# A four-layer graph network: A added to the scores on VectorE, row constants dropped, and two small sums moved to GpSimd

## The reference

```
# layer 0, h = relu(layernorm(x)), adj is A (256 x 256)
s1 = h @ (A[:, :128]).T            # by i: "U" in the kernel, bias b_lin is added
s2 = h @ (A[:, 128:]).T            # by j: "W" holds -s2
pre = s1[:, :, None, :] + s2[:, None, :, :] + b_lin
e = einsum('bije,e->bij', where(pre >= 0, pre, 0.2 * pre), a) + A
x = x + sigmoid(softmax(e, axis=2) @ h)
# layer 1
x_h = elu(h @ Wi + bi)
e = sigmoid(a_tgt[:, :, None] + a_src[:, None, :] + be) * mask
agg = e @ x_h ;  self_part = x_h * sum(e, axis=-1)
recv = elu(concat(agg, self_part) @ Wn + bn)
x = x + concat(recv, x_h) @ Wm + bm
```

## Time and profile before

| | us |
|---|---|
| median of 3 runs (5992.98 to 6012.51) | 5996.21 |
| the profiled execution, its own time | 5989.9 |
| its span, first to last instruction | 5988.1 |
| PE busy | 5885.9 (98%) |
| ACT busy | 5269.2 (88%) |
| POOL busy | 4916.4 (82%) |
| DVE busy | 4837.7 (81%) |

### The profile page before, as it was taken

The page is one execution under the profiler, slowest core; times in us unless marked ns, Lnnn a source line. Parts: engine busy times, 40 slices in busy tenths (PEclk is TensorE's granted clock), DMA queues, the critical chain, the costliest instruction groups (busy, mean ns, idle before and its releaser), DMA issues.

```text
span 5988.1 us, 128923 instructions
## 1 busy us (share of the span) xinstructions
PE 5885.9 (98%) x41812; PEld 2318.3 (39%) x41812; DVE 4837.7 (81%) x9171; ACT 5269.2 (88%) x12793; POOL 4916.4 (82%) x10392
## 2 busy tenths in 40 slices
PE   8999999999999999999999999999999999999997
PEld 2333333333334333333333333333433333333334
DVE  8978887888887888878888788888888887888873
ACT  8988898899988899888999889998889988899983
POOL 9988888888888888888888888888888888888880
PEclk9999999999999999999999999999999999999998
DMA  0000000000000000000000000000000000000000
GB/s 13 5 3 7 7 7 6 3 6 7 7 6 3 7 6 7 7 2 7 6 7 7 6 3 6 7 7 6 3 7 6 7 6 3 7 6 7 7 5 6
DMA packets 44353, 36.62 MB, mean 6 GB/s; under 512 B 4721, under 2 KB 39410, under 8 KB 43506
## 3 DMA queue, kind: packets, MB, share of 16 engines
q1 hardware_dynamic: 43506, 26.50, 1.5%
HBM read 9.71 MB, written 8.39 MB: 3 GB/s over the span
## 4 chain that ended last, share of the span: by engine, by line
PE 94%; ACT 2%; DVE 1%; POOL 1%; issue 1%; DMA 0%; SPq 0%; POOLq 0%; ACTq 0%; DVEq 0%
PE S L1015 58%; PE R L957 15%; PE S L957 6%; PE W L957 5%; PE R L1157 3%; PE PA L957 2%; ACT ring L812 2%; PE R L1165 1%; POOL ring L507 1%; PE PB L957 1%; PE S L1006 1%; PE S L1008 1%; DVE ring L613 1%; PE PB L1042 1%; PE PA L1023 0%
## 5 line engine op out<-in xcount | busy, mean ns | idle before, releaser
L507 POOL TENSOR_SCALAR ring<-W,U 128x256 f32<-128x256 f32 x9664 | 4686.4, 503 | 713.8 <-PE S L1015 642.2
L812 ACT ACTIVATE ring<-W,U 128x256 f32<-128x256 f32 x10272 | 4244.1, 503 | 13.3 <-PE S L1015 13.2
L1015 PE MATMUL S<-ring,a_window 128*32 128x512 f32 x32768 | 3750.1, 596 | 12.8 <-POOL ring L507 7.3
L613 DVE TENSOR_TENSOR ring<-U,W 128x512 f32<-128x512 f32 (+1 forms) x3840 | 3209.2, 862 | 155.5 <-PE S L1015 117.4
L1015 PEld LDWEIGHTS S<-ring,a_window 128*32 128x32 f32 x32768 | 952.2, 110 | 2269.6 <-issue 2245.4
L608 DVE TENSOR_TENSOR ring<-U,W 128x256 f32<-128x256 f32 x2464 | 993.6, 408 | 0.0
L957 PE MATMUL R<-mT,W 128*128 128x512 f32 (+1 forms) x640 | 339.1, 611 | 2.7 <-ACT mT L916 2.7
L957 PE MATMUL R<-AT,h 128*128 128x256 f32 x1260 | 316.8, 395 | 2.7 <-ACT h L928 2.1
L748 DVE SCALAR_TENSOR_TENSOR rh<-tr,h3T 128x512 f32<-128x512 f32 (+1 forms) x165 | 114.1, 692 | 240.2 <-ACT tr L919 240.2
L957 PEld LDWEIGHTS R<-AT,h 128*128 128x128 f32 x1260 | 230.4, 193 | 129.7 <-issue 100.6
L478 POOL TENSOR_TENSOR minus_mean<-mv,minus_one 128x4 f32<-128x4 f32 (+1 forms) x160 | 31.6, 197 | 272.3 <-DVE mv L676 216.8
(11 more groups left out here) (186 smaller groups left out, 4238.6 us busy)
## 6 DMA issues: line engine op xcount, KB each, us to landing
X<-in_x SPq DMA_DIRECT2D x64, 128.0 KB, 2.4
X_held<-X SPq DMA_DIRECT2D x32, 256.0 KB, 2.3
out<-OUT SPq DMA_DIRECT2D x64, 128.0 KB, 1.9
raw<-in_L_gnn_w_w SPq DMA_DIRECT2D x3, 128.0 KB
A<-in_adj SPq DMA_DIRECT2D x1, 256.0 KB, 2.7
Wn<-in_L_gnn_Wn SPq DMA_DIRECT2D x1, 128.0 KB
Wm<-in_L_gnn_Wm SPq DMA_DIRECT2D x1, 128.0 KB
rawu<-in_L_gnn_u_w SPq DMA_DIRECT2D x2, 64.0 KB
```

The costliest lines, as they stand in the source:

```text
L507: last = gp.tensor_scalar(ring[:, place, g, half * N:(half + 1) * N], W[:, y, c], LARGEST, U[:, y, c, i:i + 1], ALU.min, ALU.max)
L613: piece = dve.tensor_tensor(ring[:, place, g:g + groups].rearrange("p g (h j) -> p g h j", h=NB), u.unsqueeze(3).to_broadcast([P, groups, ...
L812: last = act.activation(ring[:, place, g, half * N:(half + 1) * N], W[:, y, c], ACT.Relu, bias=U[:, y, c, i:i + 1], scale=-1.0)
L1015: last = pe.matmul(S[y][g * ROWS:(g + 1) * ROWS, :], a_window[:, c, ROWS - 1 - row:2 * ROWS - 1 - row], ring[:, place, g], start=False, st ...
```

## The change

1. The weights `lin_w` are now 128 columns wide, the plain product of A's second half with `a`, the same for every row. One matmul of 512 columns, with H0T read twice, sets up `S`. `by_max`, `w_lin`, `A_bias` and their making are gone, and so are the one-column matmuls for `lin_i`.
2. ScalarE's blocks are relu(W - U[i]) in place of relu(U[i] - W). They differ from max(W, U[i]) by U[i], which is the same for every j of a row and so cancels in the softmax. ScalarE needs -U as its bias: VectorE makes `U_minus` (128x512) at `PRE["evacuate"]`, where it had copied `lin_i`.
3. VectorE's maximum pass becomes two passes of 128x256. Each adds A to the scores, negates, writes the result to SBUF (`neg_score`) and keeps the row's minimum (`neg_max`). The small step that made `exp_bias` is gone. ScalarE's exp reads `neg_score` with scale -1.
4. In layer 1, GpSimd adds the two halves of the edge weights (`edge_sum`), so the row sums take one matmul of 512 columns in place of four of 256. GpSimd adds bm + 0.5 to X1 (`X1_shifted`), so the four matmuls with one row of ones are gone.
5. `stage_costs` has two new costs for GpSimd, so `SHARES` changes: 403 blocks for VectorE, 298 for GpSimd, 323 for ScalarE. 45 of the 128 lots have another split.

```diff
-L1 = dict(project=26, ...
+L1 = dict(shift=22, halves=37, project=26, ...
...
+    put(pool, L1, 0, shift=13, halves=13)
...
-            gp.memset(by_max[:], 1.0).then_inc(mask_ones, 1)
...
+            def layer1(t, turn):                       # GpSimd
+                pair = turn.at(1, 0)
+                if t == L1["shift"]:
...
+                    need(gp, x2_ready, turn.at(1, -1))
+                    gp.wait_ge(x1_ready, turn.at(2, 0))
+                    gp.tensor_tensor(X1_shifted[:], X1[:], bm_half[:].unsqueeze(1).to_broadcast([P, 4, P]), ALU.add).then_inc(x1_shifted, 1)
+                if t == L1["halves"]:
+                    gp.wait_ge(edge_ready, pair)
+                    gp.tensor_tensor(edge_sum[:].rearrange("p (y n) -> p y n", y=2), edge[:, :, 0], edge[:, :, 1], ALU.add).then_inc(edge_halves, 1)
...
                 if p == PRE["evacuate"]:                # VectorE
-                    dve.wait_ge(uw_psum, value)
-                    dve.tensor_copy(lin_i[:, y], PA[:, N:N + NB])
+                    dve.wait_ge(u_ready, value)
+                    dve.tensor_scalar(U_minus[:, y], U[:, y], -1.0, None, ALU.mult).then_inc(u_minus_ready, 1)
...
                     dve.wait_ge(freed[RING - 1], lots_done)
-                    dve.tensor_reduce(neg_max[:], S[y][:].rearrange("p (r j) -> p r j", r=NB), AXIS.X, ALU.max,
-                                      negate=True).then_inc(max_ready, 1)
-                    one_piece()
-                    dve.wait_ge(max_ready, value)
-
+                    need(dve, prob_ready, value - 1)
+                    dve.memset(score_carrier[:], 0.0)
                     for r in range(NB):
-                        last = dve.scalar_tensor_tensor(exp_bias[:, r:r + 1], neg_max[:, r:r + 1], lin_i[:, y, r:r + 1],
-                                                        lin_i[:, y, r:r + 1], ALU.subtract, ALU.add)
-                    last.then_inc(exp_bias_ready, 1)
+                        last = dve.tensor_tensor_reduce(neg_score[:, r], S[y][:, r * N:(r + 1) * N], A[:, r], -1.0, LARGEST,
+                                                        ALU.add, ALU.min, accum_out=neg_max[:, r:r + 1])
+                    last.then_inc(max_ready, 1)
...
                     dve.wait_ge(out1_psum, pair)
-                    dve.tensor_tensor(X2[:], S[1][:].rearrange("p (r d) -> p r d", r=4), X1[:],
+                    dve.wait_ge(x1_shifted, pair)
+                    dve.tensor_tensor(X2[:], S[1][:].rearrange("p (r d) -> p r d", r=4), X1_shifted[:],
...
-                    act.wait_ge(u_ready, turn.at(2, y + 1))      # ScalarE, first lot of a batch
+                    act.wait_ge(u_minus_ready, turn.at(2, y + 1))
...
                     last = act.activation(ring[:, place, g, half * N:(half + 1) * N], W[:, y, c], ACT.Relu,
-                                          bias=U[:, y, c, i:i + 1], scale=-1.0)
+                                          bias=U_minus[:, y, c, i:i + 1])
...
-                        last = act.activation(prob[:, r], S[y][:, r * N:(r + 1) * N], ACT.Exp, bias=exp_bias[:, r:r + 1],
+                        last = act.activation(prob[:, r], neg_score[:, r], ACT.Exp, bias=neg_max[:, r:r + 1], scale=-1.0,
...
-                    need(pe, prob_ready, turn.at(2, y - 1))       # PE, first lot of a batch
+                    need(pe, max_ready, turn.at(2, y - 1))
...
-                    for r in range(NB):
-                        pe.matmul(S[y][:, r * N:(r + 1) * N], lin_w[:, y, r], H0T[:, y], start=r == 0, stop=False,
-                                  skip_group_check=True)
-                    pe.matmul(S[y][:].rearrange("p (r j) -> p r j", r=NB), ident[:], A_bias[:], start=False, stop=False,
+                    pe.matmul(S[y][:].rearrange("p (r j) -> p r j", r=NB), lin_w[:],
+                              H0T[:, y].unsqueeze(1).to_broadcast([P, NB, N]), start=True, stop=False,
                               skip_group_check=True)
...
-                    for r in range(NB):
-                        mm(PA[:, N + r:N + r + 1], H0T[:, y, r * P:(r + 1) * P], w_lin[:, 0:1])
...
-                    for y in range(2):
-                        for r in range(NB):
-                            last = mm(S[1][:, y * N:(y + 1) * N], ones[:], edge[:, y, r], r == 0, r == NB - 1)
-                    last.then_inc(agg1_psum, 1)
+                    pe.wait_ge(edge_halves, pair)
+                    mm(S[1][:], ones[:], edge_sum[:]).then_inc(agg1_psum, 1)
...
-                        mm(S[1][:, n * P:(n + 1) * P], ones[0:1, :], bm_half[:], True, False)
-                        mm(S[1][:, n * P:(n + 1) * P], recvT[:, n * P:(n + 1) * P], Wm[:, 0], False, False)
+                        mm(S[1][:, n * P:(n + 1) * P], recvT[:, n * P:(n + 1) * P], Wm[:, 0], True, False)
```

78 lines of the change are left out of this document (27 added, 51 removed).

## The result

| | us | ratio to before (95%) |
|---|---|---|
| before, median of 4 runs (5992.98 to 6012.51) | 5998.4 | |
| after, median of 4 runs (5901.49 to 5920.95) | 5903.9 | 0.9845 (0.982 to 0.987) |
| forecast | 5807 | 0.968 |

The change makes the kernel faster, by half of what was forecast: 94.5 us instead of some 190. The profiled execution after took 5901.5 us with a span of 5899.7, so its span is 88.4 us shorter than the 5988.1 before.

The account below looks back on a forecast made before the run. PE was taken as the bound, its feeders' lead just holding. 31 turns x 5.93 us, plus 4 and 3, less 2, gave 188.8 us off: 5801 in the profiled execution's terms, 5807 in the median's, own range 5785 to 5825.

Parts of the forecast that it names:

- Bound and PE's work: Whole loop turn: PE is the bound, so PE work removed comes off the 184.25 us turn while feeders lead.
- per-turn sum of 5.93 us: PE per turn: start of `S` 1.92, one-column matmuls 0.94, row sums 0.85, output 2.22 us; low end 5.11.
- the start of `S`: PE, twice per turn: one matmul of 512 columns stays, two of 256 go, saving 0.96 us each time.
- Rival D: Output on PE: the eight matmuls keep their spacing, 25 us less saved, 5832 us; chance 0.15.
- 1.4 us late: VectorE at the end of each half: waits for ACT's U, then negates, reaching the next lot 1.4 us late.
- So the saving just fits, with no reserve: Lot 6 at the turn's start: leads left of 0.4 us for ACT and 0.2 for VectorE; no PE idle counted.
- rival A: Lots 5 to 7: feeders' lead too short, PE waits, up to 44 us taken back, 5851 us; chance 0.18.
- the prediction's sign for A: PE idle time on the ring over 40 us in all, ahead of lots 5 to 7; forecast under 25.
- Rival B: Whole turn: ACT is the bound, turn stays 184.25 us plus ACT's extra 1 us, 6020 us; chance 0.03.
- Rival C: VectorE's row pass is slow, 4 us a pass, giving 6046 us; decides from about 3.5 us; chance 0.02.
- the 1.3 taken: VectorE's row maximum: two passes with read-outs take 1.3 us, bounds 0.8 and 2.5, 0.2 us more than before.
- Outside the loop: Start saves 4 us (3 to 5), tail 3; turn 0 and turn 1's start give nothing, may cost 2.

Follow-up runs that it names:

- after_late: Changed kernel with VectorE's U_minus two lots later, behind its blocks of lots 63 and 127: 5884.7 us (0.9814).
- late_pad100: Changed kernel with U_minus two lots later and 100 satisfied waits in TensorE's first turn, which move its loop 100 instructions on: 5833.1 us (0.9729).
- after_straight: Changed kernel with TensorE's turns written out as straight code, the other engines keeping their loops: 5846.4 us (0.9751).
- late_less_act: Changed kernel, all engines' turns written out, U_minus two lots later, ScalarE leaving out one block in seven of lots 110 to 117: 5803.5 us (0.9676).
- before_straight: Kernel before with TensorE's turns written out as straight code: 5971.2 us (0.9953).

## Why the prediction was wrong, step by step

In short: PE's work fell as forecast, but the prediction put VectorE's lateness, the loop's return and the new place of the loop at nothing, and there 3.1 us a return against the forecast were lost in each of 28 returns, 87 us.

**Bound and PE's work: right.** PE was the bound, and the per-turn sum of 5.93 us was 5.72 when measured lot by lot. The one term off is the start of `S`, 0.96 forecast and 0.86 measured: the matmul that stays takes 1.05 us to the first ring matmul (3042.24 to 3043.29), where the two of 256 columns took 0.96 (3079.63 to 3080.59). Rival D didn't happen: the eight output matmuls take 1.97 us by the fall of 2.24 from 4.21.

**"1.4 us late": the step that failed, with the next.** The prediction had VectorE 1.4 us late at the next lot by its wait for U, and costed it at nothing, since VectorE was still ahead of PE. It worked out the lead at lot 6 only. It was right about the wait (2.27 us stood ahead of this U_minus, and 0.43 us in it). At lot 127 the lead fell from 3.76 to 0.94 us. The sequencer's record of its wait for that lot stands 2.56 us ahead of the lot's first matmul in before and 2.00 us in after (medians of 28 turns), and PE has no idle time ahead of it in either: the lateness reached the sequencer and does not show as a wait of PE. No loss shows for it at any lot away from the return: outside the lots where PE's own work changed they differ by less than 0.04 us. Here a branch of 3.6 us comes next, and its cover went from 2.05 to 1.22 us. Taken away alone (after_late) this is 0.74 us a turn; by turns of after and after_late without the lower clock, 0.6.

**The return itself was not in the sum.** The row with 1.11 us of idle time "issue", one above the first of the earlier trace rows at that place, was left out of the argument, as if it were fixed. In fact the change moved the loop to a place with 20 instructions left in its first piece of code (by the estimate above), and moving it away is worth 1.6 us a turn (after_late to late_pad100): 1.8 at lots 0, 1 and 6 and 0.5 at lot 127, with 0.7 back in waits for feeders. So 2.3 us of the missing 3.1 are these two steps, with the clock's 0.2 in them.

**"So the saving just fits, with no reserve": it does not fit.** Lots 3 and 6 lack 2.1 us in after_straight, where the leads forecast for lot 6 were 0.2 and 0.4. The engine that comes last there is GpSimd, held up by VectorE's statistics, and its lead at this place was never worked out; VectorE and ScalarE are 1.3 and 1.7 us ahead at lot 6. In the changed kernel as it is this doesn't show, because the return's gap gives the feeders their time; of the 0.9 us by which late_pad100's 179.35 stays above 178.4, 0.76 are these waits. It is rival A's mechanism in part, with another engine. That its 5851 is near after_straight's 5846 is luck, since that kernel has no return and waits 2.1 us where A allowed 1.43. In after itself PE's idle time on the ring passed the prediction's sign for A, 43.0 us for "over 40", but not for A's reason: 16.0 are the stop in lot 0, and of the 26 us that went to feeders (11 before) 23 lie in turns 0 and 1 and 2 in the loop.

**Rival B** (ScalarE the bound) was wrong for the changed kernel and right about what comes next: the engine with 19.8 us of idle time a turn has none for 62 us on end, and that stretch, not the share of 90%, makes the 1.0 us that late_less_act takes away. Rival C was far off: the two passes with their read-outs take 0.8 us, less than the 1.3 taken.

**Outside the loop.** PE's first ring matmul comes at 14.2 us for 18.6 (4 forecast, 4.4 measured). The last turn and the tail behind it are 10.4 us shorter, where one turn's 5.9 and 3 were forecast. Turns 0 and 1 together took 304.6 us for 293.8: 10.8 us lost, where a loss of 2 was forecast for turn 0 and a gain of 5.9 for turn 1. In these two turns PE waits 14.8 us for VectorE's blocks (3.0 in before), and two `U_minus` of after take ten times what they take in the loop:

```profile
80.65 5.09 DVE L624 TENSOR_SCALAR U_minus<-U 128x512 f32<-128x512 f32 x1 [3.27 <-ACT U L811]
153.58 4.28 DVE L624 TENSOR_SCALAR U_minus<-U 128x512 f32<-128x512 f32 x1 [5.61 <-ACT U L811]
```

Why isn't known, and how much of the loss is the change's isn't shown: the two turns take 291.9 to 304.6 us in the changed kernels and 293.8 to 300.1 in the old one's. Of the same code, turn 1 took 149.9 us in before and 155.7 in before_straight, with a granted clock of 1.00 and 0.97:

```profile
162.90:318.60 155.70, 151.61 (x1191) 55.30 (x1190) 140.50 (x261) 146.27 (x367) 144.09 (x317) 0.97 0.02 5
```

**The account.** 188.8 us were forecast, the spans differ by 88.4. Of the 100 missing, 88 are in turns 2 to 30 (28 returns at 3.1 us are 87 of them, the start of `S` in mid-turn 3, less some small gains), 15 in turns 0 and 1, and the program's start and tail gained 2 more than forecast.

## What to carry to other kernels

Around a loop's return, count the lead of every feeder against the depth of the bound engine's queue (2.05 us of matmuls at this return), not against zero, and price the return (3.3 to 4.5 us on PE's sequencer here) as idle time that the work queued ahead of it must cover. When a kernel's code before or in a loop changes length, the place of the loop's first instruction against the 16 KB pieces changes too (100 places were worth 1.6 us a turn, after_late to late_pad100): a few satisfied waits ahead of the loop, or straight code, tell whether a disappointing result is the change's or the layout's. A wait that is moved to just ahead of an engine's own branch leaves less queued work to cover that branch (in late_pad100 VectorE had 0.43 us queued and stood idle for 2.69). A gap that hides another engine's shortage is worth only what is left when both are gone, so close both before you judge either.
